# A four-stage graph network on one core: in the first message pass, the window block moves ahead of the inverse counts

## The reference, cut to what matters

```python
def rgcn_conv(x, src, dst, etype, W, root, bias):
    seg = dst * R + etype
    agg = segment_sum(x[src], seg)           # sum over the edges of a (node, relation)
    cnt = segment_sum(ones, seg)
    agg = where(cnt > 0, agg / maximum(cnt, 1), 0)
    return einsum('nrd,rdk->nk', agg, W) + x @ root + bias
h = relu(rgcn_conv(concat(x, node_emb[node_type]), src, dst, edge_type, W1, root1, b1))
...
# a later stage: sum of edge_weight * x[src] by dst; another: attention over edges (src, dst)
```

## Time and profile before

| | |
|---|---|
| runs before, median of 3 | 5267.58 us (5249.11 to 5267.61) |
| profiled execution, own time | 5260.04 us |
| its span, first to last instruction | 5258.3 us |
| first pass, first to last cast to `rel_t` | 579.8 to 2154.3 us of the span |
| mean granted clock of TensorE | 0.823 |

### The profile page before, as it was taken

How to read it: one execution, slowest core, us unless ns; L and a number is a source line. 1 busy time by engine, 2 the same in 40 slices (tenths; PEclk the granted TensorE clock), 3 DMA queues, 4 the chain that set the end, 5 groups by cost and what they waited for, 6 DMA issues and landing times.

```text
span 5258.3 us, 105311 instructions
## 1 busy us (share of the span) xinstructions
PE 3666.9 (70%) x20468; PEld 2929.5 (56%) x20688; DVE 2687.7 (51%) x6973; ACT 1162.6 (22%) x3868; POOL 2380.1 (45%) x2346
## 2 busy tenths in 40 slices
PE   4777566666777777766767677677777777584872
PEld 1233455555666666555555555566566666574862
DVE  7654344444444444355555555455554554794336
ACT  0122111111111122122222222223322322351112
POOL 0000233344455555466666666566666665002530
PEclk8999777787888888877777778788888888797986
DMA  2022222222333444322323233344444444255740
GB/s 75 33 63 68 73 61 67 74 73 81 97 101 115 121 120 123 108 76 78 86 80 84 81 90 89 105 115 117 126 124 123 129 125 115 104 208 150 203 133 13
DMA packets 478385, 526.90 MB, mean 100 GB/s; under 512 B 96596, under 2 KB 398238, under 8 KB 474670
## 3 DMA queue, kind: packets, MB, share of 16 engines
q1 hardware_dynamic: 252780, 246.52, 15.1%
q0 software_dynamic: 85824, 199.51, 14.0%
q10 hardware_dynamic: 139746, 80.46, 5.2%
HBM read 399.82 MB, written 126.39 MB: 100 GB/s over the span
## 4 chain that ended last, share of the span: by engine, by line
PE 36%; issue 20%; POOL 14%; DMA 13%; DVE 9%; DVEq 3%; ACT 2%; ACTq 1%; SPq 1%; POOLq 0%; another core or an unknown queue 0%
POOL msg_r L608 14%; DMA msg_r<-y_tab,idx_r 9%; PE psum L1566 9%; PE psum L1636 4%; PE psum L1568 2%; DMA msg_r<-x_tab,idx_r 2%; DVE shot_r L1136 2%; PE psum L1747 2%; PE psum L1709 1%; PE psum L1432 1%; PE psum L1494 1%; DVE h_t L1365 1%; PE psum L1748 1%; PE psum L1524 1%; PE psum L1506 1%
## 5 line engine op out<-in xcount | busy, mean ns | idle before, releaser
L608 POOL DMA_INDIRECT msg_r<-y_tab,idx_r x2160 | 2221.9, 1029 | 2223.9 <-issue 1161.6
L1566 PE MATMUL psum<-shot_r 128*128 128x200 f32 x2604 | 1000.1, 486 | 465.1 <-DVE shot_r L1136 437.3
L1130 DVE SCALAR_TENSOR_TENSOR shot_r<-edge_f,win_base,iota 128x600 bf16<-128x600 f32 x434 | 366.4, 844 | 1197.1 <-PE psum L1568 740.7
L684 ACT COPY idx_r<-row_i 128x1 int32 x2142 | 395.6, 190 | 2246.6 <-DMA msg_r<-y_tab,idx_r 2044.3
L1566 PEld LDWEIGHTS psum<-shot_r 128*128 128x128 f32 x2604 | 554.8, 262 | 476.5 <-issue 472.1
L1115 DVE TENSOR_SCALAR hot_r<-iota,edge_g 128x128 f32<-128x128 f32 x1602 | 454.4, 357 | 186.4 <-PE psum L1748 148.8
L1568 PEld LDWEIGHTS psum<-shot_r 128*100 128x100 bf16 x2604 | 444.7, 171 | 115.0
L1568 PE MATMUL psum<-shot_r 128*100 128x128 bf16 x2604 | 462.3, 271 | 0.0
L1747 PE MATMUL psum<-msg_r,shot_r 128*128 128x128 f32 x1440 | 338.1, 321 | 175.3 <-DMA msg_r<-y_tab,idx_r 94.6
L1636 PEld LDWEIGHTS psum<-hot_r,msg_r 128*128 128x128 f32 x2880 | 408.9, 218 | 16.7 <-DMA msg_r<-y_tab,idx_r 6.8
L1636 PE MATMUL psum<-hot_r,msg_r 128*128 128x128 f32 x2880 | 405.8, 300 | 11.3 <-DMA msg_r<-y_tab,idx_r 4.5
(11 more groups left out here) (322 smaller groups left out, 4932.6 us busy)
## 6 DMA issues: line engine op xcount, KB each, us to landing
msg_r<-in_attr SPq DMA_DIRECT2D x882, 64.0 KB
h_t<-count_tab SPq DMA_DIRECT2D x25, 1600.0 KB, 6.6
w_tab<-shot_r ACTq DMA_DIRECT2D x385, 100.0 KB
count_tab<-shot_r ACTq DMA_DIRECT2D x385, 100.0 KB
h_t<-w_tab SPq DMA_DIRECT2D x24, 1600.0 KB, 8.0
msg_r<-y_tab,idx_r POOLq DMA_INDIRECT x2160, 2.6
xn<-heavy_tab SPq DMA_DIRECT2D x76, 320.0 KB
y_tab<-y_s SPq DMA_DIRECT2D x25, 640.0 KB, 2.9
```

Source lines behind the costliest of these rows:

```text
L608: pool.indirect_dma_start(out=msg_r[:, q, 0:width], out_offset=None, in_=table, in_offset=bass.IndirectOffsetOnAxis(ap=idx_r[:, q:q + 1], ...
L684: nc.scalar.copy(idx_r[:, q:q + 1], of[:, q:q + COLS - U + 1][:, bass.ds(c0, 1)]).then_inc(s_idx[k], 1)
L1130: V.scalar_tensor_tensor(out=key_b, in0=of(KEY, KW), scalar=win_base[:, bass.ds(w, 1)], in1=to(KW), op0=ALU.subtract, op1=ALU.is_equal).th ...
L1566: T.matmul(win_ps, low_f[:, i, :], weighted_f[:, i, :], start=False, stop=False)
```

## The change

In the first pass DVE calls `window_hots` right behind `group_columns`, ahead of its wait for the turned relations and of the cast to `rel_t`. PE calls `window_sums` ahead of `inverse_counts`. Nothing else moves, and no instruction is added or taken away in a group's work.

```diff
                 p0, p1, chunk = tile_ranges(dve, D, rest)[:3]
                 with dve.Fori(p0, p1) as p:
                     c0 = group_columns(0, D, p, chunk)
+                    window_hots(in_pass(dve, 0, p, D, None))
                     alone(dve)
                     dve.wait_ge(s_rel_ps, p)
                     V.tensor_copy(rel_t[:, :], psum[0:SPLIT * SPLIT_AT, 6, 3 * P:4 * P]).then_inc(s_rel_t, 1)
                     dve.wait_ge(s_einv_acc, p)
-                    window_hots(in_pass(dve, 0, p, D, None))
                     for h, half in halves():
...
                 x = in_pass(pe, k, p, D, n_rest) if k < 3 else None
+                if k < 3:
+                    window_sums(x)
                 if k == 0:
                     inverse_counts(p, slot)
-                if k < 3:
-                    window_sums(x)
                 for q in range(U):
```

## The result

| kernel | median, us | runs, lowest to highest | ratio to the kernel before, 95% interval |
|---|---|---|---|
| before, same chip | 5258.34 | 4, 5244.24 to 5267.61 | |
| changed | 5351.56 | 4, 5339.47 to 5355.62 | 1.0176 [1.0142, 1.0209] |

The change makes the kernel 1.76% slower. The forecast was 5330 us, 1.2% slower; the median lies inside its range. The profiled execution took 5355.62 us with a span of 5353.9 us, 95.6 above the span of the kernel before.

The account below looks back on a forecast made before the run. It took a chain between engines, no full engine, as the bound. Middle groups +30 and tile edges +34 gave +64 us on the profiled 5260.0, about 5324, said as a 5330 us median; range 5280 to 5390.

Parts of the forecast that it names:

- the new circle: First pass, middle group, scaled one-hot to next: columns, register work, window, inverse counts; 11.23 us against 10.31.
- a stall inside a tile's last group: PE reaches the turning before the next tile's columns are ready and stands 1.25 us amid its sums.
- One thing named as a sign of being wrong: Prediction wrong if middle groups' window matmuls run at full clock; one-visit middle groups were to take 11.2 us.
- the circle through the window and the scaled one-hots: The forecast case itself for the first pass: 68%, own range 5295 to 5370 us.
- G: DVE's register work between columns and one-hots in the first pass: 1.90 us; at 2.38 the middle term would be +65.
- the middle: 71 intervals between casts away from tile edges in the first pass: together +30 us.
- the rival's mechanism: TensorE's clock tips up in middle-group windows: about 25 of 71 at full clock, 42 us less, 5290 us; 14%.
- the window link: Middle group, window matmuls and close: 3.36 us at half clock, 1.68 at full; forecast kept 3.36.
- First to second group: Tile's edge: PE does inverse counts behind the window, then waits for scaled one-hots; net +1.2 us each, 24 times.
- the 0.3 it counted as saved: First to second group: some 0.3 of the 0.55 us between inverse counts and window saved, since the clear stays.
- Last to first group: Tile's edge: trade costs 1.0 to 1.1 us, PE's `y_s` wait covers the stall and shrinks 0.9; net +0.2.
- The rival that the clock tips down at the edge: PE's 1 us hole leaves half of 4 to 5 us edge work at half clock: 53 us more, 5383; 10%.

Follow-up runs that it names:

- the filler: Changed kernel plus eight 128x512 matmuls by zeros behind each window's clear, except in a tile's first group: 5292.83 us, ratio 1.006 to the kernel before.
- the clear ahead: Kernel before with DVE's first visit ahead of the cast, any second behind the scaled one-hots, and PE's inverse counts after the window's clear: 5120.23 us, ratio 0.9733.
- the late wait: Changed kernel with DVE's wait for its own columns moved behind the window's one-hots in the first pass: 5326.32 us, ratio 1.0139 to the kernel before.
- the early table: Changed kernel with ACT's copy of table rows to `y_s` ahead of a tile's last group: 5728.06 us on the slower chip, ratio 1.0066 to the kernel before.

## Why the prediction was right, and where its steps were off

**The mechanism.** The steps of the new circle show as they were said: the wait before the cast at 0, a wait for the inverse counts before the first scaled one-hot in all groups (4.00 in the example, 3.8 in the mean), PE idle 0.97 between inverse counts and sums, a stall inside a tile's last group (1.39, forecast 1.2). One thing named as a sign of being wrong came too: in 20 of the 37 one-visit groups the window ran at the full clock, and such a group takes 10.53 us in the mean, not 11.2. That the circle through the window and the scaled one-hots costs, and not the visits ahead of the cast, is shown by the two experiments on the halves: +3.8% with PE's, 2.0% faster with DVE's first visit alone (there with the second visit moved behind the scaled one-hots, so it is not DVE's half as it stands).

**G, the register work: mis-sized.** The forecast took 1.90, the same instructions as behind the cast. It measured 2.19, and 1.96 when DVE no longer waited for its own columns there. So most of the missing 0.29 is that wait. The earlier trace rows give 1.90 from the cast's end, but 2.19 from its start; that DVE's queue goes on as soon as the cast has begun, and behind the columns only when they are finished, fits both numbers and was not tested by itself. It adds 72 x 0.29 = 21 us. The Trainium skill, "Advanced Engine Details and Errata", section Sequencer Loop, whose rule would have made G nearly 0, doesn't describe this place: 2.19 us of idle DVE stand in the rows of the changed kernel.

**The clock in the middle: the rival's mechanism came too.** The forecast kept the window link as it was, "since PE still idles some 3 us ahead of the window". In the rows it idles 2.35 behind fast sums and 1.68 behind slow ones, since slow sums end later, and behind the short wait the window runs at full clock. Of the 37 one-visit windows 18 stand behind less than 1.9 us of idle PE, and 17 of these run at full clock; 19 stand behind more than 2.3, and 10 of these run at half, 6 change on the way, and 3 run at full. A group takes some 9.9 us with a window at full clock and 11.7 with one at half. With two visits that makes up to 37 us given back. So the middle is 30 + 21 - 37 = +14 by these terms; it measured +18. Two errors of the forecast nearly cancelled, and its good total there is luck in part. What the idle time does to the window is read off the rows, and only its other side, the filler, was tried: with it all 37 windows take under 1.9 us. "TensorE: Matmul & The Clock Gate", part 1, of the Trainium skill says that idle time halves the clock and activity brings it back; by this the runs agree: 0.92 granted with the filler, 0.80 without.

**First to second group: +1.46 each against 1.2, right in kind.** The sums start 1.47 behind the inverse counts (2065.02 to 2066.49 in the changed kernel), as the forecast had it (0.44 + 1.02); of the 0.3 it counted as saved, little came: in the 16 tiles with one visit there, the time from the first group's sums to the second's window is 7.81 against 7.94.

**Last to first group: this step failed.** It read: "And that wait shrinks: ACT's step hangs on gathers that the group before released, and groups now stand 0.9 further apart, so it comes 0.9 earlier seen from the sums." It came 0.8 later (5.95 against 5.16). The reason that the rows show is the clock once more: the sums ahead of the last group ran at half clock (3.78 us against 1.95 in the earlier trace rows), and the gathers start 1.3 later for it. Nor does the last group stand further off: its window at full clock brings it to 10.13 behind the one ahead in the example, where it was 10.28. The forecast took a group's distance for the gathers' start and left out that sums could be slow, though it had them so in the earlier trace rows.

The edges whose last group has one visit can be sorted by these sums. Where they were slow ahead of the last group (12 edges), the step takes 6.81 us; where they were fast ahead of it and in it, 5.55 in 2 edges here, 5.53 in 15 with the filler, and 5.36 in 13 before. The stall of 1.39 is in all of these but those of before. With the turning behind chunk 5, where there is no stall, the step behind slow sums is 6.79 in 7 edges. So the sums' clock makes some 1.3 of the step, and the stall adds nothing to it that shows.

What remains, from `heavy_sums1` to the first group's sums, grew from 8.76 to 10.35 in the mean. That isn't a dearer trade. At the full clock throughout, an edge with one visit takes 5.90 to 5.98 there before (5 edges) and 6.80 to 7.08 here (5 edges), 0.9 to 1.1 more; in the example, with the clock down in both, it is 9.02 before (1952.99 to 1962.01) and 10.05 here (2045.76 to 2055.81), 1.03 more. The forecast was 1.0 to 1.1. The rest is edge work at the lower clock: eight of these edges take 10.8 to 11.6 us at a granted clock of 0.53 to 0.61, where before none took over 9.1. The rival that the clock tips down at the edge had put such a price on the step from first to second group; there it did not come (granted clock 0.98 in the 16 tiles with one visit, 1.00 before).

In the second profile of the changed kernel the excess is 1.4 an edge, not 2.3, so this term moves between executions by some 20 us.

**The sum.** Forecast 64 and, beside the profile's own 5260, a median of 5330. Measured 95.6 between the profiles: 12 less than forecast in the middle, 6 more at first-to-second, 49 more at last-to-first, 12 that came back outside. 64 - 12 + 6 + 49 - 12 = 95.

## What to carry to other kernels

A long wait in the profile (here 293.7 us) isn't the price of what is waited for: look at what ran in its shade, and at which other step the reordering puts behind an engine's longest work. When a change has a half on each of two engines, cost and run the halves apart; here one half costs 3.8% and the other, cut so that it can stand alone, is worth 2.0%, and 2.7% with the clear ahead. In a circle between engines, an instruction that another engine waits for belongs ahead of work that nobody waits for yet.

## What the runs showed of the hardware that I had not expected

- Matmuls with zeros paid, by 1.2% with eight to a window, while PE was waiting in a circle (granted clock 0.80 to 0.92 between 1000 and 2000 us), and four to a window cost 1.0% in the version with the clear ahead, the late wait and the early table.
- The same work at a tile's edge, from `heavy_sums1` to the first group's sums, takes from 6.8 to 11.6 us within one execution of the changed kernel, at granted clocks of 1.0 and 0.56.
- A wait of an engine on its own finished instruction is visible in front of register work: 2.20 against 1.96 us, 119 times.
- The chips differ: the kernel before took 5258 us on one and 5693 us on another. The ratios taken on the slower one are therefore not compared with the others. Its four profiles show more idle time in which an engine waits for nothing that the profile shows: ScalarE 789 to 838 us, where the ten others have 575 to 624, and PE 332 to 398 against 178 to 222. What makes the chip slower stays open.
